# A state-space layer on one core: order of work in block 0, the last store, and who turns and scales x in group 0

## The reference

```
state = state * exp(dt * A) + (dt * x) outer B
y     = state . C + x * D
```

## Time and profile before

| | us |
|---|---|
| median of 3 runs | 3118.68 (3118.25 to 3118.69) |
| the profiled execution's own time | 3118.07 |
| its span, first to last instruction | 3116.3 |
| TensorE busy | 3098.2 (99%) |
| VectorE busy | 2681.8 (86%) |
| ScalarE busy | 1787.1 (57%) |
| GpSimd busy | 813.7 (26%) |

### The profile page before, as it was taken

How to read it: one execution, slowest core, us unless ns; L and a number is a source line. 1 busy time by engine, 2 the same in 40 slices (tenths; PEclk the granted TensorE clock), 3 DMA queues, 4 the chain that set the end, 5 groups by cost and what they waited for, 6 DMA issues and landing times.

```text
span 3116.3 us, 55148 instructions
## 1 busy us (share of the span) xinstructions
PE 3098.2 (99%) x17392; PEld 2547.4 (82%) x17392; DVE 2681.8 (86%) x4675; ACT 1787.1 (57%) x4782; POOL 813.7 (26%) x833
## 2 busy tenths in 40 slices
PE   8999999999999999999999999999999999999999
PEld 7788888887888888888788888888878888888887
DVE  7998888987598999999759899999975899999984
ACT  5766666664256665566326666655633656666651
POOL 4444443434022222212203122222110211221210
PEclk9999999999999999999999999999999999999999
DMA  8777777776665555565566555555646655556554
GB/s 286 277 263 274 270 271 273 261 264 248 241 228 191 195 201 188 192 203 192 181 224 205 196 193 193 202 190 190 215 164 229 212 190 196 196 195 201 192 190 163
DMA packets 185670, 672.63 MB, mean 216 GB/s; under 512 B 21056, under 2 KB 22208, under 8 KB 185408
## 3 DMA queue, kind: packets, MB, share of 16 engines
q1 hardware_dynamic: 161280, 584.91, 53.8%
q10 hardware_dynamic: 24128, 84.42, 8.3%
HBM read 532.41 MB, written 136.84 MB: 215 GB/s over the span
## 4 chain that ended last, share of the span: by engine, by line
PE 90%; DVE 6%; ACT 2%; issue 1%; DMA 1%; SPq 0%; ACTq 0%; DVEq 0%
PE dense L1157 20%; PE dense L1159 19%; PE dense L1158 19%; PE pX L1157 7%; PE pX L1159 7%; PE pX L1158 7%; PE pY L1271 3%; DVE conv_us L1572 3%; PE pD L1271 1%; PE pCB L1244 1%; PE pS L1158 1%; PE pS L1157 1%; PE pS L1159 1%; PE pU L1157 1%; PE pU L1159 1%
## 5 line engine op out<-in xcount | busy, mean ns | idle before, releaser
L1157 PE MATMUL dense<-xn_hi,w_hl 128*128 128x512 f32 (+2 forms) x2192 | 868.3, 396 | 2.2 <-ACT conv_us L725 1.3
L1159 PE MATMUL dense<-xn_hi,w_hl 128*128 128x512 f32 (+2 forms) x2192 | 853.1, 389 | 0.0
L1158 PE MATMUL dense<-xn_lo,w_hl 128*128 128x512 f32 (+2 forms) x2192 | 851.9, 389 | 0.0
L1572 DVE SCALAR_TENSOR_TENSOR conv_us<-conv_in,const_g,conv_us 128x512 f32<-128x512 f32 x576 | 469.5, 821 | 30.2 <-ACT conv_us L725 18.4
L1157 PEld LDWEIGHTS dense<-xn_hi,w_hl 128*128 128x128 f32 (+1 forms) x2192 | 409.8, 187 | 92.5 <-ACT conv_us L725 4.8
L1159 PEld LDWEIGHTS dense<-xn_hi,w_hl 128*128 128x128 f32 (+1 forms) x2192 | 409.5, 187 | 88.1
L1158 PEld LDWEIGHTS dense<-xn_lo,w_hl 128*128 128x128 f32 (+1 forms) x2192 | 410.0, 187 | 85.8 <-issue 2.6
L1607 DVE STREAM_TRANSPOSE x_tm<-xBC 32x320 f32<-32x320 f32 x832 | 417.8, 502 | 12.8
L520 POOL TENSOR_TENSOR C_lo<-xBC,C_hi 128x128 fp32r<-128x128 f32 x120 | 66.0, 550 | 1207.6 <-ACT S_hi L768 1207.2
L1757 DVE STREAM_TRANSPOSE xBC<-yn 32x256 f32<-32x256 f32 x672 | 292.9, 436 | 77.9 <-ACT yn L845 67.6
L1157 PE MATMUL dense<-z_hi,w_hl 128*128 128x512 f32 x820 | 326.5, 398 | 1.9 <-DVE acc L1780 1.1
(11 more groups left out here) (239 smaller groups left out, 5673.5 us busy)
## 6 DMA issues: line engine op xcount, KB each, us to landing
w_hl<-w_split SPq DMA_DIRECT2D x732, 512.0 KB, 3.5
w_split<-w_hl SPq DMA_DIRECT2D x244, 512.0 KB, 3.8
cum_b<-cum_scratch ACTq DMA_DIRECT2D x128, 512.0 KB, 5.0
w_raw<-w_slots_dram SPq DMA_DIRECT2D x122, 512.0 KB, 5.5
acc<-x_tr_dram ACTq DMA_DIRECT2D x16, 512.0 KB, 6.5
out_tr_dram<-acc ACTq DMA_DIRECT2D x16, 512.0 KB, 4.7
xBC<-x_tok_dram SPq DMA_DIRECT2D x6, 512.0 KB, 5.3
conv_us<-x_tok_dram SPq DMA_DIRECT2D x6, 512.0 KB, 6.1
```

The lines of the kernel that those rows point to most:

```text
L1157: nc.tensor.matmul(out, lhs[0], rhs[0], start=start, stop=False)
L1158: nc.tensor.matmul(out, lhs[0], rhs[1], start=False, stop=False)
L1159: return nc.tensor.matmul(out, lhs[1], rhs[0], start=False, stop=stop)
L1572: nc.vector.scalar_tensor_tensor(out=conv_u[r], in0=conv_in[r][:, t:t + TB], scalar=const_g[p][:, 4 * j + t:4 * j + t + 1], in1=conv_u[r], ...
```

## The change

In block 0: for group 1 (`behind_first`) ScalarE normalizes chunk 3 of group 0 ahead of emptying gate unit 1, and makes z_hi of it ahead of the split of gate 2; VectorE makes z_lo of it ahead of the lo of gate 2, and does lo(K_OUT) behind chunk_1(1). For group 7 the last three quarters of x_rows stand one place later, between the out_adds. For groups 1 to 6 VectorE's lo of conv units 2 and 5 stands between the taps of units 1 and 4 and the silu of units 0 and 3, where it stood behind gated_lo.

In the later blocks' group 0 `turned` is true for all chunks: TensorE makes no transposes for chunks 2 and 3, VectorE does a second x_rows of four quarters in four places, and ScalarE makes all four skip terms (`skip_first`). In the last block the last store is two stores of one tile.

```diff
@@ turned, xt_n
-            return g > 0 or c < 2
+            return True
...
-            before = (G - 1) + (q - 1) * (2 * (G - 1) + 1)
-            return before + (1 if g == 0 else 1 + (g - 1) * 2 + (c // 2 + 1))
+            return (G - 1) + (q - 1) * (2 * G) + g * 2 + (c // 2 + 1)
@@ ScalarE: chunk_1
                     wx_high(g, c)
+                    if g == 0 and not first_block:
+                        skip_first(c)
                     if c >= 1:
                         normalize(g, c - 1)
...
+                def skip_first(c):
+
+                    act.wait_ge(xt_done, xt_n(q, 0, c, first_block))
+                    for h in range(HPG):
+                        ins = nc.scalar.activation(xD[:, h * P:(h + 1) * P], x_tm[:, c % 2, h * P:(h + 1) * P], ACT.Copy,
                                                    scale=D_g[:, h:h + 1])
                     ins.then_inc(xd_done, 1)
@@ ScalarE: group
                         mean_square(0, 3)
-                        gate_unit(1)
+                        split(g, k_gate(first, 1))
                         normalize(0, 3)
+                        ev_gate(g, first, 1, p)
...
+                    if behind_first:
+                        z_high(0, 3)
                     split(g, k_gate(first, 2))
-                    if not first:
+                    if not first and not behind_first:
                         z_high(g - 1, 3)
@@ ScalarE: end of the block
-                store(3)
+                if last_block:
+                    store_tile(OT - 2)
+                    store_tile(OT - 1)
+                else:
+                    store(3)
@@ VectorE: skip, group
                 def skip(g, c):
+                    if g == 0 and not first_block:
+                        return
...
-                            if first_block and m < 2:
-                                x_rows(g, 2, p, 2 + m, 3 + m)
+                            row = m + (1 if last else 2)
+                            if row < 4:
+                                x_rows(g, 2, p, row, row + 1)
                             out_adds(g, m, halves=(1,))
-                            lo(g, K_OUT + m)
+                            if not (behind_first and m == 0):
+                                lo(g, K_OUT + m)
...
-                    def x_conv(j):
+                    def x_conv(j, low=None):
                         if not last:
                             conv_taps(g, j, p)
+                            if low is not None:
+                                lo(g, K_X + low)
                             if j >= 1:
                                 silu(g, j - 1, 1 - p)
...
                     masked(g, 0)
+                    if behind_first:
+                        gated_lo(0, 3)
                     lo(g, k_gate(first, 2))
...
                         router_top()
-                    else:
-                        x_rows(g, 2, p, 1, 2)
+                        if early:
+                            x_rows(0, 2, p, 0, 1)
+                    else:
+                        if not last:
+                            x_rows(g, 2, p, 1, 2)
...
                         chunk_1(g, 1)
+                        if behind_first:
+                            lo(g, K_OUT)
                         out_unit(1)
                     masked(g, 1)
                     out_unit(2)
 
                     if first:
+                        if early:
+                            x_rows(0, 2, p, 1, 2)
                         x_taps(0)
+                        if early:
+                            x_rows(0, 2, p, 2, 3)
                         x_low(0)
                     chunk_2(g, 1)
                     gated(g, 0)
...
                     state(g, 1)
                     if first:
                         x_low(1)
+                        if early:
+                            x_rows(0, 2, p, 3, 4)
                     gated_lo(g, 0)
                     chunk_1(g, 2)
...
-                        x_conv(x[1])
+                        x_conv(x[1], x[1] + 1)
                     gated_lo(g, 1)
                     if not first:
-                        x_low(x[1] + 1)
+                        if last:
+                            x_low(x[1] + 1)
                         state(g, 2)
                         x_conv(x[1] + 1)
```

More of the change, by code:

```diff
@@ L428, in _ @@
             block_body(NQ - 1, False, True)
-            sp.wait_ge(out_stored, 16 + NQ * 64)
+            sp.wait_ge(out_stored, 16 + NQ * 64 + 16)
         @block.gpsimd
@@ L822, in skip @@
                         ins = nc.scalar.activation(xD_2[c % 2][:, h * P:(h + 1) * P], x_tm[:, c % 2, h * P:(h + 1) * P], ACT.Copy,
+                                                   scale=D_g[:, h:h + 1])
+                    ins.then_inc(xd_done, 1)
+                def skip_first(c):
+                    act.wait_ge(xt_done, xt_n(q, 0, c, first_block))
+                    for h in range(HPG):
+                        ins = nc.scalar.activation(xD[:, h * P:(h + 1) * P], x_tm[:, c % 2, h * P:(h + 1) * P], ACT.Copy,
                                                    scale=D_g[:, h:h + 1])
@@ L1091, in block_body, with store_tile @@
                 (group if first_block else paired_group)(7, 1, last=True)
+                def store_tile(i):
+                    act.wait_ge(evac_dve, tail_n(q, i))
+                    act.dma_start(out_tr[bass.ds(q, 1), :, i:i + 1, :].rearrange("b p o t -> (b p) o t"),
+                                  acc[:, i:i + 1, :]).then_inc(out_stored, 16)
                 def store(m):
```

## The result

The changed kernel takes 3146.94 us (median of 4 runs, 3145.66 to 3148.80), the kernel before 3118.58 beside it on the same chip: a ratio of 1.0087 [1.0075, 1.0099], so slower by 28.4 us. The forecast was 3144.0. The profiled execution took 3146.92, its span is 3145.1 (before 3116.3), and the mean granted clock of TensorE is 0.997 instead of 1.000.

The account below looks back on a forecast made before the run. TensorE, busy 99%, was taken as the bound, so other engines' lead over it decides. Profiled 3118.07 +22.2 (later blocks) +4.2 (block 0) −0.4 (store) = 3144.1, say 3144; range 3123 to 3153, the forecast's own 3133 to 3151.

Parts of the forecast that it names:

- the five waits: TensorE's forecast waits in later blocks' group 0, at pY(1), pS(2), pY(2), pD(1), pD(2): 1.75, 1.85, 0.9, 1.8, 1.5 us.
- First stall, 1.75: Later blocks' group 0: VectorE waits 3.8 us for skip_first(1), so masked(1) is late and TensorE waits 1.75 at pY(1).
- pS(2) 1.85, pY(2) 0.9, pD(1) 1.8, pD(2) 1.5: Later blocks' group 0: TensorE's next waits in us, for S_lo, masked(2), normalize(1) and normalize(2), all late.
- Group 1, 0.9: Later blocks' group 1: VectorE still lags, so z_lo of chunk 3 comes late and costs another 0.9 us a block.
- Later blocks +22.2: Blocks 1 to 3 together: 7.6 us lost in each of blocks 1 and 2, 7.0 in block 3.
- Gate unit 1, +6.0: Block 0, groups 1 to 6: low parts ahead of the silus delay evac(5); 1.0 us a group, bounds 0 and 7.
- Group 1 of block 0, −1.0: Earlier normalize, z_high and gated_lo end waits on yn and z_lo, acc's grows: 1.0 us gained, bounds −2 and 0.
- Group 7, −0.8: Block 0, group 7: one transposed quarter behind out_adds(0) removes a wait on acc; 0.8 us gained with its restart.
- Last store, −0.4: End of the last block: tile 6 leaves earlier and tile 7 goes alone; 0.4 us gained, between 0.1 and 1.3.
- Rival A: Faster: VectorE's extra work is covered and block 0's order costs nothing; 3113 us, chance 0.12.
- rival B: Half: short wait for skip_first(1), only VectorE's lag of some 6 us; 1 to 3 a block, 3121 to 3131, chance 0.16.
- rival C: Worse: lag not absorbed in group 1 and stretching returns; 10 us a block or more, 3152 to 3160, chance 0.07.

Follow-up runs that it names:

- experiment 1: Changed kernel with the lo of conv units 2 and 5 back behind gated_lo in block 0's groups 1 to 6: 3139.91 us, ratio 1.0066.
- experiment 3: Changed kernel with all four skips of the later blocks' group 0 back on VectorE, which still turns all chunks: 3135.93 us, ratio 1.0052.
- experiment 6: Changed kernel with only conv unit 5's lo put back in block 0's groups 1 to 6: 3142.11 us, ratio 1.0072.
- experiment 7: Kernel before plus split last store, group 7's order and group 1's earlier normalize, z_high, gated_lo; lo(K_OUT) in its old place: 3117.55 us, ratio 0.9992.
- experiment 8: experiment 7 plus all chunks turned in later blocks' group 0, skips 0, 1 on VectorE, 2, 3 on ScalarE, silu(0) behind masked(2): 3130.20 us.
- experiment 2: Changed kernel with group 0 of the later blocks as before, block 0 and stores still changed: 3123.81 us, ratio 1.0012.
- experiment 4: Changed kernel with TensorE's transposes for chunks 2 and 3 as before and ScalarE making only skips 0 and 1: 3123.87 us, ratio 1.0012.

## Why the prediction was right

Slower by 25.3 was forecast, 28.4 measured, inside the forecast's own range; the mechanism of the later blocks is the one predicted, link by link. The sum in them is closer than its terms: the five waits are 0.2 less than forecast, group 1 gives 0.5 less, and the slower start behind each wait gives 0.6 more.

- **First stall, 1.75.** Measured 1.88. The idle time of VectorE ahead of x_tm was to be 3.8 and is 3.08, as VectorE was through the router later than forecast. The prediction's own times, 893.4 and 891.81, make 1.6 and not 1.75, and its other four stalls are 0.05 to 0.1 above their differences; it does not say what this extra is.
- **pS(2) 1.85, pY(2) 0.9, pD(1) 1.8, pD(2) 1.5.** At full clock (experiment 1, block 2): 2.22, 0.48, 1.63, 1.40. The five are 7.8 forecast, 7.6 measured. In the changed kernel the last is missing, as the clock's fall, which the prediction did not have, fills its place. That this left the sum as it was is luck: in experiment 3, where TensorE had less to wait for, a fall did cost time.
- **Group 1, 0.9.** It did not come in the changed kernel. In experiment 1, pD(2) stands 7.1 behind (1705.51 − 922.37 − 769.15 − 6.89) and the block ends 7.5 behind, so 0.4.
- **Later blocks +22.2.** Measured 22.6 (7.7, 7.5, 7.5). The forecast's 7.0 for block 3, with no wx in its last chunk, measured 7.5.
- **Gate unit 1, +6.0.** At gate unit 1 itself 5.9. The six groups lose 7.3, over the upper bound of 7: the 1.3 at a conv unit are a wait that the prediction did not have. It stays in experiment 6 and is gone in experiment 1, so it is unit 2's lo. The 0.1 taken off for less stretching of taps(4) was not there: in group 1 they take 3.14 (L1594 above), 3.08 before. The forecast wait of 1.3 to 1.6 at gate unit 1 measured 1.05 to 1.33.
- **Group 1 of block 0, −1.0.** This step failed: +0.6. It let the later wait on acc grow by only a part of the 1.3 won; experiment 7 shows that all of it goes (0.75 on the weights' low part, 0.5 more on acc), since VectorE's add comes no earlier. The 0.6 on top are longer durations in VectorE's list ahead of that add: 0.2 go with the moved lo(K_OUT), 0.4 with a load of weights that landed later, and experiment 8 has 0.6 with lo(K_OUT) in its old place. The step's upper bound, 0, was no bound.
- **Group 7, −0.8.** Measured −1.0.
- **Last store, −0.4.** Measured −0.6. The Trainium skill (DMA: Bandwidth & Descriptors, cost components) gives an estimated 0.6, and the trace agrees with it better than with the 0.4 taken from the nearest rows. The page fits its formula to transfers issued by GpSimd; these stores are ScalarE's.
- Block 0 in all: +4.2 forecast, +6.8 measured. These 2.6 are nearly the whole of the difference between 3144 and 3146.94; group 1 is 1.6 of them, the conv unit 1.3. The changed kernel's block 0 is one of the longest of the five with the same code, which lie 5.5 to 6.9 above before; so up to 1.4 of the 2.6 can be scatter.

Against the change the prediction also weighed a page: The Trainium skill (ScalarE: Activation LUTs, Rules for kernel authors) would give the eight skips an estimated 2.8 us. They took 2.02, 0.24 apart, so the row was the one to go by.

Rival A, all covered, falls with the first wait; rival B's short wait for skip_first(1) is not there either (3.08); rival C's stretching is there (three taps of 3.25), but it was there before (3.12), at another place, and adds nothing to the chain's sum.

## What to carry to other kernels

When an engine is busy 99% of the time, ask of each moved instruction not what it costs but how much lead its engine has over the busy one at that place: 3.5 us of lead does not hold a wait of 3.08 and a quarter of 2.05, though ScalarE's skips cost nothing alone and VectorE is idle for 14% of the span. Look at what stands behind the moved instruction on its engine: two low parts of 0.6 us, each ahead of a silu, cost 1.2 us in each of six groups. A shift of half a microsecond in one place is not yet an effect of the edit: the same code of block 0 took up to 1.4 us more or less from kernel to kernel, and a second kernel with the same code there is what told the two apart. And where a loss and a fall of the clock come together, look for a run or a block without the fall before counting both.

## What was not expected of the hardware

TensorE's granted clock fell to 0.50 (1.2 GHz) in group 0 of the later blocks, behind waits of 2.22 and 0.48 us of TensorE. The same waits in block 2 of experiment 1 (2.22, 0.48, 1.63) and in block 2 of experiment 6 (2.21, 0.48, 1.64) brought no fall; in block 1 of experiment 1 it fell at 893, right behind the wait of 1.88, as the 32 small matmuls of pY(1) began, and stood at 0.50 for 894:896. The kernels without such waits (experiments 2, 4 and 7) kept 1.00 throughout, and so did experiment 8 with waits of 0.63, 0.44 and 1.26 in group 0 of block 1; experiment 3 fell with 0.62 and 1.91. In the changed kernel the fall cost 0.2 us a block or less, since TensorE would have waited anyway; in experiment 3, where it had less to wait for, matmuls that start 0.43 apart instead of 0.23 cost 1.6 us in block 1, of which an estimated 1.1 would not have been waited for anyway.
